# GpSimd's chain for both norms moved ahead of the issue of the next adj, its reader waits moved to the power

## What is computed

```python
x = x + gat(_layernorm(x), adj, W, a)
x = x + moe(_layernorm(x), ...)

def gat(h, adj, W, a):
    Wh = h @ W.T
    e = leaky_relu((Wh @ a1)[:, :, None] + (Wh @ a2)[:, None, :], 0.2)
    attention = softmax(where(adj > 0, e, -9e15), axis=-1)
    return elu(attention @ Wh)
```

## Time and profile before

| | us |
|---|---|
| median of 3 runs | 298.63 (297.75 to 301.1) |
| the profiled execution, its time | 300.65 |
| the profiled execution, its span | 298.9 |
| busy in the span: PE, DVE, ACT, POOL | 263.3, 241.8, 229.9, 165.4 |

### The profile page before, as it was taken

The page is one execution under the profiler, slowest core; times in us unless marked ns, Lnnn a source line. Parts: engine busy times, 40 slices in busy tenths (PEclk is TensorE's granted clock), DMA queues, the critical chain, the costliest instruction groups (busy, mean ns, idle before and its releaser), DMA issues. The chain is left out here.

```text
span 298.9 us, 7855 instructions
## 1 busy us (share of the span) xinstructions
PE 263.3 (88%) x1958; PEld 237.2 (79%) x1959; DVE 241.8 (81%) x689; ACT 229.9 (77%) x498; POOL 165.4 (55%) x392
## 2 busy tenths in 40 slices
PE   7696978998889888988897798999999999999990
PEld 5576968897878877978796685689999999999990
DVE  4587899999999999999798976565768787778766
ACT  2366578989989988899788875779779888788670
POOL 3686467686667666876845852114443244432375
PEclk9979799999999999999999899999999999999998
DMA  6999432556367556665301000465464655556313
GB/s 105 174 293 168 66 43 69 98 112 152 71 143 168 113 118 155 140 136 138 83 0 37 35 1 0 164 218 168 142 186 153 201 174 169 175 170 198 107 37 105
DMA packets 47070, 37.26 MB, mean 125 GB/s; under 512 B 2849, under 2 KB 41153, under 8 KB 47041
## 3 DMA queue, kind: packets, MB, share of 16 engines
q1 hardware_dynamic: 38176, 27.49, 29.1%
q0 software_dynamic: 8864, 9.45, 20.4%
HBM read 29.57 MB, written 4.20 MB: 113 GB/s over the span
## 5 line engine op out<-in xcount | busy, mean ns | idle before, releaser
L1450 PE MATMUL banks<-whx,prob_t 128*128 128x129 f32 x512 | 65.6, 277 | 0.0
L1450 PEld LDWEIGHTS banks<-whx,prob_t 128*128 128x128 f32 x512 | 61.7, 194 | 0.0
L1434 PE MATMUL banks<-ident,logit 128*128 128x128 f32 x256 | 40.1, 292 | 19.3 <-DVE logit L701 18.2
L1153 ACT ACTIVATE leaky<-masked_dst,shift_neg 128x512 f32<-128x512 f32 x64 | 44.5, 722 | 8.9 <-POOL shift_neg L512 8.9
L1434 PEld LDWEIGHTS banks<-ident,logit 128*128 128x128 f32 x256 | 29.8, 148 | 26.7 <-DVE logit L701 17.8
L701 DVE SCALAR_TENSOR_TENSOR logit<-masked_dst,shift_pos,leaky 128x512 f32<-128x512 f32 x64 | 47.4, 749 | 4.3 <-ACT leaky L1153 3.8
L1183 ACT ACTIVATE prob_t<-banks 128x512 f32<-128x512 f32 x64 | 36.9, 606 | 11.9 <-PE banks L1434 11.7
L689 DVE CUSTOM_DVE_ANT_0 masked_dst<-mask,banks 128x512 f32<-128x512 bf16 x64 | 42.2, 682 | 2.1 <-PE banks L1411 1.0
L1319 ACT ACTIVATE logit<-logit,nb,rstd 128x128 f32<-128x128 f32 x60 | 24.8, 484 | 15.1 <-POOL nb L611 15.1
L606 POOL TENSOR_SCALAR veps<-mv 128x4 f32<-128x4 f32 x15 | 5.8, 387 | 48.9 <-DVE mv L1020 45.3
L1623 PEld LDWEIGHTS banks<-w2s,masked_dst 128*128 128x128 f32 x256 | 29.8, 192 | 0.6
(11 more groups left out here) (172 smaller groups left out, 577.5 us busy)
## 6 DMA issues: line engine op xcount, KB each, us to landing
adj_sb<-in_adj_dram POOLq DMA_DIRECT2D x16, 512.0 KB, 5.8
w_pair<-w_parts SPq DMA_DIRECT2D x31, 256.0 KB, 2.7
x_all<-in_x_dram SPq DMA_DIRECT2D x16, 256.0 KB, 4.5
w2r<-in_L_ffn_W_dram SPq DMA_DIRECT2D x32, 128.0 KB, 2.1
out_dram<-prob_t SPq DMA_DIRECT2D x15, 256.0 KB, 2.3
x_all<-x2s SPq DMA_DIRECT2D x13, 256.0 KB, 2.3
x_rows<-in_x_dram SPq DMA_DIRECT2D x8, 256.0 KB, 3.1
w_parts<-in_L_ffn_W_dram SPq DMA_DIRECT2D x1, 1024.0 KB, 9.0
```

What stands on the lines that cost most here:

```text
L1153: nc.scalar.activation(leaky[:, t, :], masked_dst[:, t, :], ACT.Identity, bias=shift_neg[:, t:t + 1], scale=ALPHA).then_inc(s_leaky, 1)
L1434: last = nc.tensor.transpose(lt_ps[t % 2][:, c * P:(c + 1) * P], logit[:, t, c * P:(c + 1) * P], ident[:])
L1450: last = nc.tensor.matmul(into[:, 0:D + 1], prob_t[:, t, c * P:(c + 1) * P], whx[par][:, c, 2:WHX], start=(c == 0), stop=(c == T - 1))
```

## The change

`norms(n+2)` is called ahead of `load_adj(n+2)` in POOL's step, and within `norms` the waits on the readers of the old factors (`s_wh`, `s_x2a`) stand no longer ahead of the first sum but ahead of the power. No arithmetic is added or removed, and the other engines' streams are the same. The first three calls (`load_adj` of batches 0, 1 and 2 with their norms) keep their order; the new order begins with POOL's step 1.

```diff
@@ -447,15 +447,11 @@
                 if past(half, b, 1):
                     pool.wait_ge(s_norm, base)
                 if first:
-                    if past(half, b, 2):
-                        pool.wait_ge(s_wh, T * (b - 1))
                     pool.wait_ge(s_bn1, T * b + T)
                 if second:
                     b2n = b - NORM_LAG
                     if past(half, b2n, 1):
                         pool.wait_ge(s_n2, 3 * b2n)
-                    if past(half, b2n, 2):
-                        pool.wait_ge(s_x2a, (T - V) * (b2n - 1))
                     pool.wait_ge(s_bn2, T * b2n + T)
                 waits_met(pool)
@@ -480,6 +476,11 @@
                     nc.gpsimd.tensor_scalar(nm2[:], nm2[:], -0.5, 0.0, ALU.mult, ALU.add).then_inc(s_n2, 1)
+                if first and past(half, b, 2):
+                    pool.wait_ge(s_wh, T * (b - 1))
+                if second and past(half, b - NORM_LAG, 2):
+                    pool.wait_ge(s_x2a, (T - V) * (b - NORM_LAG - 1))
+                waits_met(pool)
                 pool.wait_ge(s_norm, base + 6)
                 nc.gpsimd.tensor_tensor(rstd[:, kinds, :], sums[:, 1, kinds, :],
@@ -542,10 +543,10 @@
             def step(half, n):
+                if in_range(half, n + 2, KEPT - 1 + NORM_LAG):
+                    norms(half, n + 2)
                 if in_range(half, n + 2) and past(half, n + 2, 2):
                     load_adj(half, n + 2)
-                if in_range(half, n + 2, KEPT - 1 + NORM_LAG):
-                    norms(half, n + 2)
                 if in_range(half, n):
                     row_shifts(half, n)
```

## The result

The changed kernel takes 297.4 us in the median of 19 runs (295.78 to 298.92), the kernel before 299.09 us in 19 runs on the same chip (297.44 to 301.1). The ratio is 0.9945, its 95% interval 0.9923 to 0.9967, so the change is worth 1.6 us, between 1.0 and 2.3 by the interval. Forecast were -1.9 us, and no change larger than 1%. The profiled execution took 298.8 us with a span of 297.1, where before had 300.65 and 298.9: -1.8 us in the span.

What follows compares the result with a forecast made beforehand. DVE is nearly full (19.08 of 20 us); POOL's order makes the norms and `nb` late, losing 3.12 us in ten steps. -3.12 + 1.2 - 0.4 + 0.4 = -1.9 us gives 296.7, range 294.9 to 299.6.

Steps and rivals of the forecast that it cites:

- The norms' start: POOL's chain: first sum starts some 0.25 us behind the first norm's statistics, power at 102.0, 1.3 us ahead of before.
- Bias and x2s: POOL and ACT: `nb` done between 104.05 and 104.5 instead of 105.78; x2s's wait for it goes away every step.
- The issue and the shifts: POOL: adj's issue ends between 105.1 and 105.55, then `src_alpha` and `z_max`; leaky 0.5, 0.37 or 0.17 us ahead of mask.
- the middle case: POOL's shifts: `src_alpha` caught by DVE's residual, `z_max` 0.2 us earlier, leaky 0.37 ahead of mask, about 0.12 us a step.
- The price: DVE's ten steps: late leaky costs about 0.12 us each, so 1.2 of the 3.12 us lost stay.
- The last loop step: Leaky of batch 13, idle 0.40 us for `shift_neg`: the same shift of 0.4 is worth 0.4 us.
- The start: POOL's start: sums held by DVE, adj's issue later, first shift sum later; cost 0 to 0.9 us, taken as 0.4.
- adj: Load of adj: issued about 104.5, lands 5.8 us after issue, at 110.3; over 7 us of cover left before its mask.
- The full gain: Rival, 27%: issue ends before DVE's maximum, every step 9.47 us, start costs nothing; 3.5 us gained, giving 295.1.
- The issue in the place of the late bias: Rival, 24%: `row_shifts` late in every step rather than `nb` in every other; 299.9 us, with half the lateness 298.5.
- Wrong in kind?: Two signs: DVE's own instructions grow longer beside POOL's sums, or POOL's issue is held by DVE.
- the prediction's rival in which the power slips behind a logit: Rival, 8%: sums take over 4.15 us, power begins at 103.3, `nb` held by second residual; +5 us, 303.6.

Runs made afterwards that it cites:

- e1: Kernel before with the new order alone (norms, adj, row_shifts), the waits staying ahead of the first sum: 307.8 us, ratio 1.0277.
- e2: Kernel before with the moved waits alone, the issue of adj staying ahead of norms: 299.08 us, ratio 0.999.
- e3: Changed kernel with load_adj behind row_shifts instead of between norms and row_shifts: 297.17 us, ratio to before 0.9925.
- e7: Changed kernel with the old order in POOL's step 1 and all five engines' attention steps written out: 299.58 us, ratio to before 0.9953.
- e4: Changed kernel with the old order in POOL's step 1 alone (adj of batch 3 ahead of its norms): 296.34 us, ratio to before 0.9894.
- e8: Changed kernel with three small POOL instructions on unread tiles ahead of row_shifts: 300.17 us, ratio to before 1.0016.
- e5: Changed kernel with DVE's attention steps written out instead of looped: 297.99 us, ratio to before 0.9942.
- e9: e4 with load_adj behind row_shifts in steps 2 to 11, ahead of it in steps 12 and 13: 295.9 us, ratio to before 0.9912.
- e6: Changed kernel with PE's attention steps written out instead of looped: 299.39 us, one run.

## Why the prediction was right, and where by luck

**The norms' start, right.** The first sum starts 0.35 us behind the end of the statistics (0.3 forecast), is held by mask and logits, and the power starts 4.04 us behind the mask (about 4). `whx` had ended 2.1 us before it, so the moved wait costs nothing. e1 and e2 show that both halves are needed, which the prediction had implied and not said.

**Bias and x2s, right.** `nb` is 1.7 us earlier (1.3 to 1.7 forecast), and x2s never waits for it.

**The issue and the shifts, right in kind.** The issue ends 7.39 us behind the mask (7.1 to 7.5), `src_alpha` is caught by the residual as in the middle case, and leaky leads the mask by 0.41 and 0.32 us in the loop, where I took 0.37. In the written-out steps the lead is 0.47 to 0.50 and nothing is lost. The difference is POOL's own time without an instruction: 0.48 ahead of the issue in the loop, where the estimate had 0.17.

**The price, right in sum and wrong in its parts.** I put 1.2 us on late shifts in ten steps. Lost were 96.18 - 94.70 = 1.48. By e3 only 0.7 of it comes from the issue ahead of the shifts; the other 0.77 is mostly the every-second-step rest, of which the prediction knew nothing (e7: it goes when no engine loops). It was hidden in before, where the long step absorbed it: I had read the short step of one parity (9.47) as what DVE needs in both, and with the loops it needs 9.71 in the other (e3). Reading the price of a lead of 0.4 us by drawing a line between steps of different parity mixed the two: in after, a lead of 0.41 goes with 9.79 us, and one of 0.32 with 9.63. That the two errors cancel to within 0.3 us is luck.

**The last loop step, right in sign.** -0.61 for -0.4.

**The start, right in kind, its size by luck.** +0.43 for +0.4, on an estimate of 0 to 0.9 and from one execution of each kernel; over nine executions POOL's own stretch is 0.2 to 1.4 us longer in the new order. What held POOL was the mask on `src_alpha` (0.60 us) and `w_parts` on a sum, both of which the prediction had near this place. The prediction had no term for TensorE's clock, which moves the same stretch by up to 0.9 us. That e4's start is shorter than before's too (21.79 for 22.39), with the same order on POOL in step 1, I had not seen: in before the sum behind the issue was held 1.26 us by `w_parts`, in e4 three sums pass first. It is a matter of half a microsecond in where the two engines meet.

**adj, right.** It lands 7.2 us after its issue in the median (5.8 in the earlier trace rows), which the 7 us of cover that were left still carry; no mask of the loop waits for it:

```profile
adj_sb<-in_adj_dram POOLq DMA_DIRECT2D x16, 512.0 KB, 7.2
```

**The rivals.** The full gain would have needed e3's order and the missing rest. The issue in the place of the late bias would have shown steps of 9.8 or more throughout; they were 9.62 and 9.79, a good part of the way. Its 298.5 for half the lateness doesn't follow from the prediction's own terms, which give 297.8 (2.1 - 3.12 - 0.2 + 0.4 on 298.63); no other number rests on it. The power never slipped behind the last logit: it was 0.78 us ahead of it in the step shown (91.16 against 91.94).

**Wrong in kind?** Neither sign appeared. DVE's instructions kept their lengths beside POOL's sums (masks 0.68, residuals 0.69), and the issue of adj took 0.84 to 0.86 us in every step of after. Where it lies under the mask it was held: to 1.13 us in the row of e3. That agrees with what the Trainium skill, SBUF — State Buffer, SBUF: two separate sides, says of a DMA issued from GpSimd beside a DVE instruction in a two-port mode. In after the issue of the start ended at 25.54, only 0.11 us into the mask of 25.43, so there was nothing to hold; what the mask held was `src_alpha` behind it.

## To carry to other kernels

Where an in-order engine serves another in every step, ask of each wait in front of a chain whether the chain's first instruction needs it or only the one that overwrites; moving the wait and moving the chain pay only together. Read what a step needs from both steps of a loop of two: here one needed 9.47 us and the other 9.71. Where one delay makes a step long and thereby heals itself, a lateness in every step cost about half of its price times the count (e8). And before two stretches are compared, look at the granted clock in both.

## What the hardware showed unexpectedly

**TensorE's clock decides about 2 us of this kernel, whatever the change.** Two stretches of 4 us that start 9 and 13 us behind the last mask (columns as in the earlier trace rows), in after:

```profile
163.39:167.39 4.00, 2.09 (x17) 1.61 (x16) 3.67 (x14) 2.99 (x7) 3.34 (x10) 1.00 0.17 66
167.39:171.39 4.00, 3.86 (x19) 3.63 (x20) 2.96 (x6) 2.82 (x7) 3.46 (x3) 0.59 0.00 0
```

And in e4:

```profile
162.72:166.72 4.00, 2.08 (x17) 1.61 (x16) 3.66 (x14) 3.00 (x7) 3.35 (x10) 1.00 0.17 66
166.72:170.72 4.00, 3.87 (x33) 3.62 (x34) 3.96 (x14) 3.61 (x10) 3.46 (x3) 1.00 0.00 2
```

In the first stretch the two are alike: PE is busy 2.09 and 2.08 us. In the second after gets 0.59 of its clock, so most of it at 1.2 GHz instead of 2.4, with 19 matmuls in the records where e4 has 33 at 1.00. The eleven profiled executions fall into three groups by the time behind the last mask: 140.8 or 140.9 us in e1, e4 and e8, where the clock stays up from 150 to 290 us; 142.3 to 142.8 in before, after, e2, e3, e5 and e9, where it falls once between 165 and 174; 144.6 in e6 and e7, where it falls at 195 or 196 behind a long wait for weights. The same program falls on either side from run to run. Of 62 runs of before on these chips, 18 with a mean granted clock below 0.98 have a median span of 298.8 us, and 11 with one above 0.994 one of 296.1. Compared among runs below 0.98, after has 296.9 (7 runs), e9 295.3 (3), before 298.8: the change is then worth 1.9 us. From 0.98 to 0.986 it is 2.5 us (297.6 and 295.1), about 0.99 2.3 us (296.9 and 294.6); above 0.994 before has 11 runs and after none.

**POOL's small instructions are held to the end of DVE's two-input instruction; the power only if it begins under one.** The second sum of 0.2 us takes 0.77 beside a logit (87.82) and 1.18 beside `w_parts` (21.38). The power of 128x8 takes 1.66 us where a logit begins 0.78 behind it (91.16, logit 91.94), and the logit keeps its 0.75. It is held too if it begins under the logit, as twice in before (2.10 and 2.21 us, of 11):

```profile
73.25 0.75 DVE L701 SCALAR_TENSOR_TENSOR logit<-masked_dst,shift_pos,leaky 128x512 f32<-128x512 f32 x1
73.32 2.21 POOL L484 TENSOR_TENSOR rstd<-sums,minus_half 128x8 f32<-128x8 f32 x1
```

A power of 128x4 that the mask met 0.72 us behind its start took 1.45 us for 1.04 (before, 24.66 and 25.38). The longer powers bear out a premise of the prediction's rival in which the power slips behind a logit; in after the margin was the 0.78 us. In sum POOL is busy 8.6 us more in after than before for the same work, and no other engine's busy time grows.
